# Loading blocks 10 and 11 of x in one transfer, in a normalise-and-scan kernel

## The reference

```python
def step(prev, x_i):
    y = jnp.einsum('oc,nch->noh', Wc, prev) + conv_b[None, :, None]
    y = jnp.where(y >= 0, y, prelu_a * y)
    cur = y + x_i
    return (cur, cur)
x = jnp.moveaxis(feature, 3, 0)
_, fwd_rest = jax.lax.scan(step, x[0], x[1:])
fl = jnp.concatenate([x[0:1], fwd_rest], axis=0)
_, bwd_rest = jax.lax.scan(step, fl[-1], fl[:-1], reverse=True)
...
x = x + _L0_conv_ref(_gn(x), L0_conv_conv_w, L0_conv_conv_b, L0_conv_prelu_a)
```

## Time and profile before

| | us |
|---|---|
| median of 3 runs | 376.47 (376.31 to 376.53) |
| the profiled execution | 376.38 |
| its span | 374.6 |
| TensorE passes busy | 351.7 (94%), 3100 |
| VectorE busy | 286.0 (76%) |
| ScalarE busy | 230.0 (61%) |
| POOL busy | 17.3 (5%) |
| transfers of x | 5 of 1536 KB, 3 of 768 KB, 1 of 512 KB, 7 of 256 KB |

### The profile page before, as it was taken

One profiled execution on the slowest core, in us unless ns is written; L12 is line 12 of the kernel. 1 busy time (PEld: TensorE's weight loads), 2 busy tenths in 40 slices (PEclk: granted clock), 3 DMA queues, 4 the chain that ended last, 5 costly groups with the idle time before them and its releaser, 6 DMA issues.

```text
span 374.6 us, 10099 instructions
## 1 busy us (share of the span) xinstructions
PE 351.7 (94%) x3100; PEld 350.6 (94%) x3100; DVE 286.0 (76%) x925; ACT 230.0 (61%) x810; POOL 17.3 (5%) x30
## 2 busy tenths in 40 slices
PE   0279999999999999999999999999999999999996
PEld 0179999999999999999999999999999999999996
DVE  2688899788887887665666878778778787787786
ACT  2886656656556566565565665655656657566564
POOL 2078000000000000000000000000000000000000
PEclk9999999999999999999999999999999999999999
DMA  8998000000000000000000121211212212122122
GB/s 308 429 412 308 2 0 1 0 0 0 1 0 0 1 0 0 0 0 0 0 0 0 59 84 56 84 66 73 84 56 84 82 58 84 61 79 84 56 112 84
DMA packets 10088, 26.30 MB, mean 70 GB/s; under 512 B 1248, under 2 KB 1504, under 8 KB 9440
## 3 DMA queue, kind: packets, MB, share of 16 engines
q1 hardware_dynamic: 10080, 26.22, 18.1%
HBM read 13.63 MB, written 12.58 MB: 70 GB/s over the span
## 4 chain that ended last, share of the span: by engine, by line
PE 91%; DMA 6%; SPq 1%; DVE 1%; ACT 1%; issue 0%; ACTq 0%
PE psum L352 88%; DMA xin<-in_x 6%; PE psum L312 1%; SPq L234 1%; PE psum L302 1%; DVE state L535 0%; DVE state L530 0%; ACT state L382 0%; ACT state L376 0%; PE psum L277 0%; PE psum L273 0%; PE psum L266 0%; ACT above L445 0%; PE psum L295 0%; PE psum L289 0%
## 5 line engine op out<-in xcount | busy, mean ns | idle before, releaser
L352 PE MATMUL psum<-state,w_t 128*128 (+1 forms) x2976 | 332.6, 275 | 0.0
L352 PEld LDWEIGHTS psum<-state,w_t 128*128 128x128 f32 x2976 | 332.5, 192 | 0.0
L445 ACT ACTIVATE above<-psum,params 128x128 f32<-128x128 f32 x376 | 139.7, 372 | 129.6 <-PE psum L352 128.7
L530 DVE TENSOR_TENSOR state<-above,state 128x128 f32 (+1 forms) x376 | 108.4, 288 | 66.1 <-ACT above L445 56.4
L447 ACT ACTIVATE below<-psum,negative 128x128 f32<-128x128 f32 x376 | 139.9, 372 | 0.0
L535 DVE SCALAR_TENSOR_TENSOR state<-below,negative,state 128x128 f32 (+1 forms) x376 | 123.4, 349 | 6.7
L582 DVE TENSOR_TENSOR state<-state,xin (+1 forms) x45 | 30.8, 684 | 0.0
L475 DVE TENSOR_SCALAR state<-xin,mean,rstd 128x320 f32<-128x320 f32 (+2 forms) x72 | 27.9, 435 | 0.0
L457 DVE BATCH_NORM_STATS2 bstat<-xin 128x6 f32<-128x512 f32 x32 | 20.0, 672 | 8.7 <-DMA xin<-in_x 8.7
L266 PE MATMUL psum<-chan,centre 128*128 128x64 f32 (+1 forms) x8 | 2.1, 361 | 18.7 <-DVE chan L471 18.7
L266 PEld LDWEIGHTS psum<-chan,centre 128*128 128x128 f32 x8 | 1.6, 251 | 19.0 <-issue 15.5
(11 more groups left out here) (38 smaller groups left out, 24.6 us busy)
## 6 DMA issues: line engine op xcount, KB each, us to landing
out_y<-state SPq DMA_DIRECT2D x47, 256.0 KB, 2.0
xin<-in_x SPq DMA_DIRECT2D x5, 1536.0 KB, 12.8
xin<-in_x SPq DMA_DIRECT2D x3, 768.0 KB, 21.8
xin<-in_x SPq DMA_DIRECT2D x7, 256.0 KB, 18.1
w_t<-in_w SPq DMA_DIRECT2D x4, 256.0 KB, 10.6
xin<-in_x SPq DMA_DIRECT2D x1, 512.0 KB, 24.1
out_y<-state SPq DMA_DIRECT2D x1, 192.0 KB, 1.9
out_y<-state SPq DMA_DIRECT2D x1, 64.0 KB, 1.6
```

What stands on the lines that cost most here:

```text
L352: mm = nc.tensor.matmul(psum[:, 4 * par + o, 0:COLS], w_t[:, k, o * P:(o + 1) * P], xs[k], start=k == 0, stop=k == 3)
L445: nc.scalar.activation(above[:, par, o, :], z, ACT.Relu, bias=params[:, o:o + 1], scale=1.0).then_inc(above_done, 1)
L530: nc.vector.tensor_tensor(sts[o], above[:, par, o, :], sts[o], ALU.add).then_inc(part_done, 1)
```

## The change

The two blocks become a sixth pair. The transfers of blocks 10 and 11 become one, and both blocks share one semaphore, as those of the other pairs do.

```diff
-PAIRS = {0: 1, 2: 3, 4: 5, 6: 7, 8: 9}
+PAIRS = {0: 1, 2: 3, 4: 5, 6: 7, 8: 9, 10: 11}
```

## The result

| | before | after |
|---|---|---|
| median of 16 runs, us | 376.51 (376.31 to 376.76) | 377.27 (376.99 to 377.48) |
| ratio, 95% interval | | 1.0020 (1.0013 to 1.0027) |
| the profiled execution, us | 376.38 | 377.23 |
| its span, us | 374.6 | 375.2 |
| start of the step loop L352 in it | 38.93 | 39.52 |

The kernel is 0.76 us slower. I take the span first.

What follows compares the result with a forecast made beforehand. TensorE, busy for 94% of the span, was taken as the bound, so only a later first product of block row 3 counts: 376.47 + 0.78 = 377.25 us, the 0.1 pace gain included. The range was 376.5 to 377.7.

Steps and rivals of the forecast that it cites:

- which I cost at nothing: SP's queue: one load issue, some 0.5 us, goes away; counted as no change in time.
- signs of being wrong: Listed observations: block 10 before 25.2, POOL's last power by 36.0, 24 passes over 3.5 us, or L352's shift unlike the total.
- Pace: Transfer queue: the pair lands at 25.53, 0.1 us earlier than block 11 did; bounds 0 to 0.2.
- The added wait: Block 10 on ScalarE and VectorE: both wait until 25.54 for the pair, having started at 24.45 and 24.57 before.
- The term of 0.04: ScalarE's group values of batch 1 (L402): 0.04 us was a wait of their own, so they move +1.11, to 26.77.
- (c): POOL's chain to the last power: +1.11 us less 0.32 idle before that power, giving +0.79.
- (b): VectorE's chain to the first product of row 3: +0.88 us at block 14's aggregate, +0.76 behind batch 3's L277.
- (a): ScalarE to TensorE: deviations of batch 2 and the 24 keep-up passes go +0.63 us, ending near 33.2.
- Cover by the wide rows: Rival: the pair lands at about 24.7, nobody waits for block 10, and the time is 376.1 us; chance 5%.
- Partial absorption: Rival: POOL's and VectorE's chains have unseen slack, so the front gives +0.4 us, 376.9; chance 18%.
- TensorE's clock: Rival: the lower clock level holds through the 24 keep-up passes, giving 379.6 us; chance 8%.

Runs made afterwards that it cites:

- e4: Kernel before with no pairs at all: blocks 0 to 12 each in a 768 KB transfer with its own semaphore; +0.74 us against before, ratio 1.0021.
- e3: Kernel before with one wait added: POOL begins batch 1's power only after ScalarE's squares of block 10; +0.74 us against before, ratio 1.0020.
- e2: Changed kernel with ScalarE's group values of batch 1 ahead of its mean of block 10; +0.69 us against the kernel before, ratio 1.0017.
- e6: Same kernel as e2, run and profiled a second time; +0.60 us against the kernel before, ratio 1.0018.
- e12: Kernel before with the last two parts of the weights in one transfer, so 20 loads; +0.15 us against before, ratio 1.0004.
- e11: Changed kernel with its parameter load in two transfers of 64 partitions, so 21 loads; +0.52 us against the kernel before, ratio 1.0015.
- e5: Changed kernel unaltered, run and profiled a second time beside the kernel before; +0.80 us against before, ratio 1.0019.

## Why the prediction was right, and where it was not

The time, the range and the direction were right: 377.25 against 377.27. That they meet to 0.02 is luck, since two errors cancel. I had +0.78 in the front, and the front gave +0.6; 0.15 to 0.2 came from around the span, which I had taken to stay as it was. That step, adding the shift of the front to the median as it stands, failed: "which I cost at nothing" is what I wrote of the issue that goes away. One of my own signs of being wrong came with it: L352 moved by 0.59, another amount than the total.

- **Pace.** I took 0.1 us from the waits; 0.07 came in the profile, and e4 shows 0.11 for two blocks inside the queue.
- **The added wait.** Block 10 on VectorE: 25.54 forecast, 25.54 measured. ScalarE woke at the same moment, 25.54, not 0.06 later.
- **ScalarE.** The group values were to be at 26.77 and were at 26.60. The term of 0.04 was mis-sized: before, L402 stood 1.21 behind the start of the mean, after it 1.06. So 0.15 of the 1.21 had been a wait for L277, not 0.04; the accumulator read of the mean starts at 26.51 and L402, which doesn't need it, 0.09 later, and I had used the 0.22 of an instruction that does (L382 of block 8, 23.08 after 22.86). POOL therefore had +0.92 in place of +1.11, and chain (c), 0.92 - 0.32 = 0.60 in place of 0.79. With the 0.06 of the wake that is 0.17 of the 0.19 between the two shifts, and this chain is the one that the front goes by.
- **VectorE.** I let block 10's aggregate wait for the squares until 28.31; it ran at 28.13, at the end of VectorE's own units. From there to the aggregate of block 14 took 4.62 us in place of 4.84, which I had moved unchanged. So (b) was +0.48, not +0.88. The 0.22 came back in small pieces: the two aggregates took 0.30 in place of 0.36, the five units behind them 3.00 in place of 3.07, the next unit 0.64 in place of 0.69. Whether these instructions were faster or held waits too short for the view, I have not tested.
- **Which chain is last.** (a) +0.45, (b) +0.48 at the aggregate of block 14 and +0.39 at L295 (35.35 after 34.96), where I had +0.76, and (c) +0.59 in the profile. I had (b) and (c) tied; it is POOL's, shown by L512's wait, by e3, and by e2, which takes it away.
- **The rivals.** Cover by the wide rows: the pair gains 0.07 to 0.11, the wait costs 0.6. The 2.0 us of fixed cost for a transfer that the Trainium skill fits (DMA: Bandwidth & Descriptors, the anatomy of one DMA), for transfers issued from GpSimd where these are SP's, does not show in this full queue: five transfers more in e4 cost 0.78 us in all. Partial absorption came half true: the front grew by 0.6, midway between its +0.4 and my +0.78, by the terms above, and the time did not stay at 376.9. TensorE's clock did not fall: the 24 passes took 2.90 in both kernels. Where it did matter was in the other direction, in e2 and e6: when it rises.

## What to carry to other kernels

Two transfers joined into one give the first half's data up to the time of the second half's landing; weigh that delay, on every engine that would have used the first half, against the gain in pace, here 1 us of delay against 0.1. A wait added to an engine delays what stands behind it in its program order too: here a small instruction for another batch, and through it POOL, busy for 5%, which had 0.32 us to spare. The idle time before the last instruction of a chain is its slack, and a delay injected into that chain alone (e3) measures it.

## What the runs showed of the hardware that I had not expected

- The time around the profiled span depends on the program: 1.82 us with 21 loads and 1.96 with 20 on one chip (before and e12), and 1.82 with 21 against 1.99 to 2.01 with 20 in kernels with the pair (e11 against e5 and the pair). The mechanism is open.
- The moment at which TensorE's clock rises in the front differs between executions of one kernel by enough to move L277 by 0.27 us (e2 and e6). In the kernel before it rose at about 27.3, in the pair's profile before 25.7, after passes that began at 22.5 in both. It moves the time only where an instruction on the path stands behind those passes.
- Behind other transfers in the queue two narrow ones cost 0.11 us more than one wide one of the same bytes (3.77 against 3.66); at the head of the queue the same split cost 0.34 (e4). Why, no run shows.
